# Two attentions of a four-stage transformer stack: the value products move from the end of a step to its middle and lag by two steps instead of one

## The chip, the cores and the metric

One core of one Trainium2 chip runs the whole program. The metric is the device time of one execution in microseconds; it is given as the median of several executions. The granted TensorE clock over the profiled execution is 0.971 of full speed, and 1.00 in both attention stages.

## What is computed

The reference is a stack of four residual layers, each `x = x + layernorm(f(layernorm(x)))`, over two sequences of 1024 tokens with 512 features:

```python
x = x + _layernorm(_L0_attn_ref(_layernorm(x), w_q, w_k, w_v, w_o))   # 32 heads of 16, full softmax
x = x + _layernorm(_L0_ffn_ref(_layernorm(x), ...))                   # gated MLP, 512 -> 1376 -> 512
x = x + _layernorm(_L1_attn_ref(_layernorm(x), Wqkv, Wo))             # 32 query heads, ONE key/value head, ALiBi, causal
x = x + _layernorm(_L1_ffn_ref(_layernorm(x), ...))                   # linear layer plus clamped low-rank adapter
# an attention, for each head: softmax(q k^T / 4 [+ alibi, causal]) v, then an output product
```

The change touches both attentions, and nothing of the rest.

## The kernel before

Each attention is one call of `attention`, with tag B (layer 0, full) or G (layer 1, `causal`). Its main loop runs over **steps**. Four heads form a group (`it`, 16 of them: 2 sequences x 8 groups). A group's queries come in two halves of 512; one group and half is a **turn** `t = 2*it + half` (32 turns). A turn is cut into key tiles `kt` of 128 keys. One step is one (`it`, `half`, `kt`). Layer 0 has 8 steps in each turn, 256 in all, all of full width. Layer 1 has 4 steps in an even turn and 8 in an odd one, 192 in all; tiles on the diagonal are narrower (512, 384, 256 or 128 queries), wide and narrow steps alternate, and each diagonal key product is followed by two small mask products (`mask_keys`, L1043).

The work of a step, by engine:

- **TensorE, key products** (`key_scores`, L1032), four a step, one for each head: scores with keys on partitions, into a ring of `n_st = 3` PSUM banks (`st_ps`). Key product n waits until ScalarE has used number n-3 (`st_used`). It is complete, and `st_made` counts it, only after its masks if it has any.
- **ScalarE, exponentials** (`exps`, L906), one for each key product, in the same order, into `probs`, a ring of three steps (`ring = 3`).
- **TensorE, row products** (`row_scores`, L1021): scores with queries on partitions, for the row maxima of a turn that comes later. A unit is one head and 128 queries; a wide one has two products (parts 0 and 1). Four PSUM banks (`s_ps`) hold two wide units. In layer 0 a step has two units.
- **VectorE, maxima** (`maximum`: L952 in layer 0, L949 in layer 1), one for each unit; it frees the unit's banks (`maxed`).
- **TensorE, value products** (`values`, L1065): for each of four heads `o_ps += v_ones x probs`, all into the one bank 7 that gathers a turn's output. Each is written to the trace as two instructions, so a step's group has 8.
- Once in a turn: `copy_o(t)` copies the finished bank 7 to SBUF (VectorE L958 in layer 0, ScalarE L913 in layer 1). The first value product of the next turn (`kt == 0`) waits for it (`o_out`). `invert` (L964) is a small reciprocal on VectorE, in the second step of a turn.
- Once in a turn: `turn_max(t)` (L1053) transposes the maxima through the same ring `st_ps`, ScalarE reads it twice (`take_max`, L895 and L896), and four small DMAs (L701, on SP's queue) write the maxima as rows of the query stack; the first key product of turn t waits for them (`m_rows`). In layer 0 `turn_max` stands at the end of the sixth step of the turn before, so the first key product that needs it is two whole steps later.

Key and row products contract over about 50 rows and sit in the upper or the lower half of the array; `step_order` interleaves the two halves so that one of each half can run at once. A step of layer 0 is, in order, K0, R(A,0), K1, R(A,1), R(B,0), K2, R(B,1), K3 with units A and B; the value products of the step before follow at the end. The order within each engine is this written order; semaphores alone tie the engines together. In the last 8 steps of an attention there are no row products, and pieces of the output product (`out.tile_piece`, L74 to L76) take their place.

In the main loop of TensorE before the change:

```python
for kind, *which in step_order(i):
    ...                       # key, row and mask products of step i
if i:
    values(i - 1)             # waits st_used for the exponentials of step i-1, o_out where kt == 0
...
for t in turn_after.get(i, ()):
    turn_max(t)
```

Of the kernel before, what the change touches and what calls it, by code (L numbers as in the profile page):

```python
# [47 lines left out]
SIDES = P // SIDE  # L48
GS = GH // SIDES
LEAD = 3400  # L50
TILES_AHEAD = 4
ROW_FIXED, STEP_FIXED = 140, 370
LOWEST = -3.0e38
# [440 lines left out]
def attention(nc, fixed_sb, step_sb, turn_sb, sems, tag, banks, causal, proj, qparts, kparts, vrows, out, nxt, turns,  # L494
# [23 lines left out]
    s_ps, st_ps, o_ps = banks[:, 0:4, :], banks[:, 4:4 + n_st, :], banks[:, 7, :]  # L518
# [61 lines left out]
    def step_order(i):  # L580

        _, _, _, first, diagonal = steps[i]
        keys = [[h for h in range(GH) if h // GS == u] for u in range(SIDES)]
        lists = [[], []]
        todo = units_at[i]

        def add_key(u):  # L590
            h = keys[u].pop(0)
            lists[u] += [("key", h)] + [("mask", h, a) for a in range(2) if diagonal]

        for j, n in enumerate(todo):
            u = units[n][2] // GS
            lists[u] += [("row", n, k) for k in range(len(row_parts(*units[n][:2])))]
            for _ in range(GH * (j + 1) // len(todo) - GH * j // len(todo)):
                add_key(1 - u if keys[1 - u] else u)
        while any(keys):
            add_key(0 if len(keys[0]) >= len(keys[1]) else 1)  # L600

        out, free = [], [0, 0]
        while any(lists):
            u = 0 if lists[0] and (free[0] <= free[1] or not lists[1]) else 1
            item = lists[u].pop(0)
            out.append(item)
            if item[0] == "row":
                x, y = row_parts(*units[item[1]][:2])[item[2]]
                free[u] += y - x
            else:  # L610
                free[u] += HALF - first if item[0] == "key" else SIDE * (item[2] + 1)
        return out
# [15 lines left out]
    tiles_ahead = TILES_AHEAD  # L628
# [47 lines left out]
    with nc.Block() as block:  # L676
# [210 lines left out]
        @block.scalar  # L887
        def _(act):
            def take_max(t):
                n = where["max", t, 0]  # L890
                act.wait_ge(st_made, n + 1)
                if t:
                    act.wait_ge(m_rows, n_rows * t)
                turned = st_ps[0:UNITS, n % n_st, 0:P]
                act.activation(mparts[:, 0, :], turned, ACT.Copy, scale=-1.0).then_inc(m_high, 1)  # L895
                act.activation(mrow[:, :], turned, ACT.Copy, scale=-1.0).then_inc(st_used, 1)  # L896

            def exps(i):
                first = steps[i][3]
                order = heads_of(i)  # L900
                for h in order:
                    n = where["exp", i, h]
                    act.wait_ge(st_made, n + 1)
                    if h == order[0] and i >= ring:
                        act.wait_ge(pv_done, i - ring + 1)
                    act.activation(probs[:, (i % ring) * GH + h, first:HALF], st_ps[:, n % n_st, first:HALF],  # L906
                                   ACT.Exp).then_inc(st_used, 1)

            def copy_o(t):
                act.wait_ge(pv_done, first_of[t + 1])  # L910
                if t >= 3:
                    act.wait_ge(o_stored, 16 * (t - 2))
                act.activation(ob[:, t % 3, :], o_ps[:, :], ACT.Copy).then_inc(o_out, 1)  # L913

            proj.scalar(act)
            for kind, n, *c in ahead:
                if kind == "out" and c[0] == DC - 1:
                    proj.copy(act, NB - 1, n)
                elif kind == "turn":
                    take_max(n)  # L920
            for i, (it, half, kt, *_) in enumerate(steps):
                exps(i)
                if causal and kt == 0 and i:
                    copy_o(2 * it + half - 1)
                for t in turn_after.get(i, ()):
                    take_max(t)
                if tile_at(i, -2) is not None:
                    out.tile_high(act, tile_at(i, -2), divided, TURNS // BATCH // 2)
            if causal:
                copy_o(TURNS - 1)  # L930
            for t in range(tiles_ahead + 2, NT):
                out.tile_high(act, t, divided, TURNS // BATCH // 2)
                nxt.scalar_tile(act, t)
            nxt.scalar(act, out)

        @block.vector
        def _(dve):
# [39 lines left out]
            for i, (it, half, kt, *_) in enumerate(steps):  # L977
                for n in units_at[i]:
                    maximum(n)
                if i - 1 == first_of[2 * it + half] and 2 * it + half >= 3:  # L980
                    invert(2 * it + half - 3)
                if not causal and kt == 0 and i:
                    copy_o(2 * it + half - 1)
                if i - first_of[last] in (3, 5):
                    invert(last - 2 + (i - first_of[last] - 3) // 2)
                if tile_at(i, -1) is not None:
                    out.tile_low(dve, tile_at(i, -1))
                if tile_at(i, 2) is not None:
                    out.tile_stats(dve, tile_at(i, 2), s_ps)
                if tile_at(i, 3) is not None:  # L990
                    out.tile_norm(dve, tile_at(i, 3), s_ps)
                if tile_at(i, 4) in range(TB - 1):
                    nxt.stats_tile(dve, tile_at(i, 4), out)
# [17 lines left out]
        def _(pe):  # L1011
# [75 lines left out]
            for i, (it, half, kt, *_) in enumerate(steps):  # L1087
                if kt == 0:
                    pe.wait_ge(m_rows, n_rows * (2 * it + half + 1))
                if i == tiles_at:  # L1090
                    pe.wait_ge(maxed, len(units))
                tile, odd = divmod(i - tiles_at, 2)
                keys, tile = 0, tile if 0 <= tile < tiles_ahead else None
                for kind, *which in step_order(i):
                    if kind == "row":
                        row_scores(*which)
                    elif kind == "key":
                        key_scores(i, *which)
                        keys += 1
                        if keys == 2 and tile is not None:  # L1100
                            out.tile_piece(pe, tile, 2 * odd, s_ps)
                    else:
                        mask_keys(i, *which)
                if i:
                    values(i - 1)
                if tile is not None:
                    out.tile_piece(pe, tile, 2 * odd + 1, s_ps)
                for t in turn_after.get(i, ()):
                    turn_max(t)
            values(len(steps) - 1)  # L1110
            for t in range(tiles_ahead, NT):
                for c in range(DC):
                    out.tile_piece(pe, t, c, s_ps)
# [798 lines left out]
```

## Time and profile before

| | us |
|---|---|
| median of 3 executions | 2115.2 (2108.39 to 2123.23) |
| the profiled execution | 2104.26 |
| its span, first to last instruction | 2102.4 |
| main loop of attention B (first to last value product) | 192.9 to 874 |
| main loop of attention G | 1431.5 to 1914 |

Times are microseconds, unless marked ns. Engines: PE = TensorE matmul, PEld = TensorE weight load, DVE = VectorE, ACT = ScalarE, POOL = GpSimd, SP = SyncE with a queue of DMA issues. L12 is line 12 of the kernel. Matmuls are pipelined and overlap in pairs, so the start times of successive matmuls tell more than their durations, and a PE that is shown as busy may be waiting inside the shadow of the matmul before. `x8` after a group is the number of instructions in it; in square brackets stands the idle time of the engine before it and what ended it.

### The profile page before, as it was taken

The numbers are of one execution on the slowest core, as the hardware profiler recorded it, in microseconds if no ns is written. First come the engines' busy times: TensorE is split into PE (matmuls) and PEld (weight loads), VectorE is DVE, ScalarE is ACT, GpSimd is POOL, SyncE is SP. The second block draws the span as 40 slices with busy tenths as digits, with TensorE's granted clock in tenths as the row PEclk, the third lists the DMA queues.
The fourth block names the chain that finished last, engine by engine and source line by source line (L and its number), as shares of the span: only waits on it lengthen the run. The fifth ranks groups of instructions, "written<-read, shape, count | busy, mean of one in ns | idle before, by whom it ended". The sixth has DMA issues, their size and how long they took to land. (4 is left out here: it accounts for less than half of the span.)

```text
span 2102.4 us, 31922 instructions
## 1 busy us (share of the span) xinstructions
PE 1911.8 (91%) x11664; PEld 1083.4 (52%) x11664; DVE 1424.3 (68%) x2446; ACT 1141.7 (54%) x2393; POOL 225.7 (11%) x275
## 2 busy tenths in 40 slices
PE   5999999999999999969999998599999999998665
PEld 4865333333333333548888886464444444445454
DVE  5346999998999898554423333567787778765457
ACT  3224888887887788514222221226777777764133
POOL 0000000110000000330001010000012000014213
PEclk9999999999999999989999999799999999999788
DMA  6582544354435530262011000563445434412411
GB/s 206 157 192 72 79 76 92 65 85 78 77 57 86 79 73 22 69 200 91 1 41 36 5 21 11 167 154 80 85 112 92 91 78 87 91 45 88 150 41 60
DMA packets 133820, 178.18 MB, mean 85 GB/s; under 512 B 50164, under 2 KB 61300, under 8 KB 133520
## 3 DMA queue, kind: packets, MB, share of 16 engines
q1 hardware_dynamic: 131360, 169.09, 35.3%
q0 software_dynamic: 2304, 7.06, 1.1%
q8 instruction: 92, 1.51, 0.3%
q14 instruction: 64, 0.52, 0.1%
HBM read 111.21 MB, written 64.36 MB: 84 GB/s over the span
## 5 line engine op out<-in xcount | busy, mean ns | idle before, releaser
L952 DVE TENSOR_REDUCE maxesB<-banksB 128x1 f32<-128x1024 f32 x512 | 602.0, 1216 | 86.2 <-PE banksB L1021 86.1
L906 ACT ACTIVATE probsB<-banksB 128x512 f32<-128x512 f32 x1024 | 529.6, 602 | 127.9 <-PE banksB L1032 127.8
L949 DVE CUSTOM_DVE_ANT_0 junkG<-banksG,rampG 128x896 bf16<-128x896 f32 (+7 forms) x512 | 367.9, 756 | 98.4 <-PE banksG L1021 92.9
L1032 PE MATMUL banksB<-q_stackB,k_stackB 50*128 50x512 f32 x1024 | 403.1, 470 | 4.8 <-ACT probsB L906 2.1
L906 ACT ACTIVATE probsG<-banksG 128x512 f32<-128x512 f32 (+3 forms) x768 | 326.1, 492 | 117.1 <-PE banksG L1043 66.1
L1021 PE MATMUL banksB<-k_stackB,q_stackB 48*128 48x512 f32 x1024 | 343.6, 441 | 3.8
L1032 PEld LDWEIGHTS banksB<-q_stackB,k_stackB 50*128 50x128 f32 x1024 | 166.5, 184 | 265.6 <-ACT probsB L906 231.3
L1032 PE MATMUL banksG<-q_stackG,k_stackG 54*128 54x512 f32 (+3 forms) x768 | 258.4, 412 | 22.4 <-ACT probsG L906 16.5
L1065 PE MATMUL banksB<-probsB,v_onesB 128*32 128x512 f32 x2048 | 273.6, 606 | 0.0
L1021 PE MATMUL banksG<-k_stackG,q_stackG 52*128 52x512 f32 (+3 forms) x768 | 247.0, 407 | 9.1 <-DVE maxesG L949 8.8
L1021 PEld LDWEIGHTS banksB<-k_stackB,q_stackB 48*128 48x128 f32 x1024 | 153.5, 185 | 85.5 <-DVE maxesB L952 74.7
L1032 PEld LDWEIGHTS banksG<-q_stackG,k_stackG 54*128 54x128 f32 x768 | 126.0, 185 | 104.7 <-ACT probsG L906 75.8
L1021 PEld LDWEIGHTS banksG<-k_stackG,q_stackG 52*128 52x128 f32 x768 | 125.3, 185 | 94.8 <-DVE maxesG L949 63.6
L1452 DVE SCALAR_TENSOR_TENSOR hD<-banksB,suD,siluD 128x512 f32<-128x512 f32 (+1 forms) x44 | 33.0, 750 | 207.7 <-PE banksB L76 190.9
L1065 PE MATMUL banksG<-probsG,v_onesG 128*32 128x512 f32 (+3 forms) x1536 | 164.5, 500 | 0.1
L1043 PE MATMUL banksG<-masks,halves 64*128 64x64 bf16 (+1 forms) x1024 | 119.0, 210 | 0.0
L1422 ACT ACTIVATE siluD<-banksB,sgD 128x512 f32<-128x512 f32 (+1 forms) x44 | 30.3, 688 | 131.4 <-PE banksB L76 131.3
L1431 ACT ACTIVATE hhD<-hD 128x512 fp32r<-128x512 f32 (+1 forms) x44 | 27.8, 632 | 114.4 <-DVE hD L1452 114.4
L76 PE MATMUL banksB<-xhTD,wgu2D 128*128 128x512 f32 x192 | 74.9, 390 | 0.0
L829 POOL TENSOR_TENSOR mpartsB<-mrowB,mpartsB 16x128 fp32r<-16x128 f32 x32 | 14.5, 453 | 562.4 <-ACT mrowB L896 562.4
L74 PE MATMUL banksB<-xhTD,wgu2D 128*128 128x512 f32 x192 | 74.8, 390 | 0.0
L75 PE MATMUL banksB<-xlTD,wgu2D 128*128 128x512 f32 x192 | 74.7, 389 | 0.0
(279 smaller groups left out, 2788.6 us busy)
## 6 DMA issues: line engine op xcount, KB each, us to landing
q_stackB<-q_parts SPq DMA_DIRECT2D x96, 128.0 KB, 7.1
k_stackB<-k_parts SPq DMA_DIRECT2D x96, 128.0 KB, 7.5
q_stackG<-q_parts SPq DMA_DIRECT2D x96, 128.0 KB
q_parts<-partsA SPq DMA_DIRECT2D x16, 512.0 KB, 4.1
k_parts<-partsA SPq DMA_DIRECT2D x16, 512.0 KB, 2.8
turns<-o_copyB SPq DMA_DIRECT2D x32, 256.0 KB, 2.2
q_parts<-partsF SPq DMA_DIRECT2D x16, 512.0 KB, 2.8
turns<-o_copyG SPq DMA_DIRECT2D x32, 256.0 KB
```

The source lines that it names most:

```text
L74: pe.matmul(out, left[0], right[0], start=start, stop=False)
L75: pe.matmul(out, left[0], right[1], start=False, stop=False)
L76: return pe.matmul(out, left[1], right[0], start=False, stop=stop)
L906: act.activation(probs[:, (i % ring) * GH + h, first:HALF], st_ps[:, n % n_st, first:HALF], ACT.Exp).then_inc(st_used, 1)
L949: dve.tensor_tensor_reduce(junk[:, n % JUNK, 0:width], scores, ramp[:, SEQ - width:SEQ], 1.0, LOWEST, ALU.add, ALU.max, out).then_inc(maxe ...
L952: dve.reduce_max(out, scores, AX.X).then_inc(maxed, 1)
L1021: ins = pe.matmul(s_ps[:, slot_of[n] + part, 0:b - a], qst[at, it % 3, half, h % GS, qt * P:(qt + 1) * P], kst[at, it % 3, h % kh, a:b], s ...
L1032: ins = pe.matmul(st_ps[:, n % n_st, first:HALF], kst[at, it % 3, h % kh, kt * P:(kt + 1) * P], qst[at, it % 3, half, h % GS, first:HALF], ...
L1043: ins = pe.matmul(st_ps[:, n % n_st, first:first + wide], halves[at, a, :], masks[at, a, 0:wide], start=False, stop=a == 1)
L1065: ins = pe.matmul(o_ps[32 * h:32 * h + 32, first:HALF], vone[:, it % 2, kt, h % vh, :], probs[:, (i % ring) * GH + h, first:HALF], start=k ...
L1422: act.activation(self.silu[0:k, :], self.g_ps[0:k, :], ACT.Silu, scale=self.sg[0:k, j:j + 1]).then_inc(self.silu_out, 1)
L1452: dve.scalar_tensor_tensor(out=self.h[0:k, :], in0=self.u_ps[0:k, :], scalar=self.su[0:k, j:j + 1], in1=self.silu[0:k, :], op0=ALU.mult, o ...
```

## The change

The value products leave the end of the step. They now stand in its middle, ahead of the third key product (or ahead of part 0 of a row unit where that stands directly before the third key product), and they are those of step i-2. After the loop the last two steps' value products follow. The first output piece of a step follows the value products. `copy_o(t)` moves from the first step of the next turn to its second, in ACT's and in DVE's order. The rings keep their sizes.

```diff
+VALUES_BEHIND = 2
...
-                if causal and kt == 0 and i:
+                if causal and i - first_of[2 * it + half] == 1 and 2 * it + half:
                     copy_o(2 * it + half - 1)
...
                 if i - 1 == first_of[2 * it + half] and 2 * it + half >= 3:
                     invert(2 * it + half - 3)
-                if not causal and kt == 0 and i:
+                if not causal and i - first_of[2 * it + half] == 1 and 2 * it + half:
                     copy_o(2 * it + half - 1)
...
-                keys, tile = 0, tile if 0 <= tile < tiles_ahead else None
-                for kind, *which in step_order(i):
+                tile = tile if 0 <= tile < tiles_ahead else None
+                order = step_order(i)
+                middle = next(n for n, item in enumerate(order) if item[0] == "key" and sum(
+                    o[0] == "key" for o in order[:n]) == 2)
+                if middle and order[middle - 1][0] == "row" and order[middle - 1][2] == 0:
+                    middle -= 1
+                for n, (kind, *which) in enumerate(order):
+                    if n == middle:
+                        if i >= VALUES_BEHIND:
+                            values(i - VALUES_BEHIND)
+                        if tile is not None:
+                            out.tile_piece(pe, tile, 2 * odd, s_ps)
                     if kind == "row":
                         row_scores(*which)
                     elif kind == "key":
                         key_scores(i, *which)
-                        keys += 1
-                        if keys == 2 and tile is not None:
-                            out.tile_piece(pe, tile, 2 * odd, s_ps)
                     else:
                         mask_keys(i, *which)
-                if i:
-                    values(i - 1)
                 if tile is not None:
                     out.tile_piece(pe, tile, 2 * odd + 1, s_ps)
                 for t in turn_after.get(i, ()):
                     turn_max(t)
-            values(len(steps) - 1)
+            for i in range(len(steps) - VALUES_BEHIND, len(steps)):
+                values(i)
```

## Rows read from the trace of the kernel before

**Rows 1.** Busy time of each engine in the two attention loops (columns are in the header).
```profile
core 0: us, PE busy (x) PEld busy (x) DVE busy (x) ACT busy (x) POOL busy (x), PEclk, DMA share, GB/s
192.90:854.90 662.00, 655.72 (x4048) 242.69 (x4047) 593.98 (x558) 529.27 (x1061) 54.46 (x80) 1.00 0.41 71
1431.40:1907.00 475.60, 446.41 (x4081) 221.74 (x4083) 360.69 (x998) 345.72 (x849) 54.18 (x86) 1.00 0.41 83
```

**Rows 2.** Timeline of PE over two steps of attention B: start, length, what.
```profile
571.76 0.50 PE L1032 MATMUL banksB<-q_stackB,k_stackB 50*128 50x512 f32 x1
...
572.70 0.39 PE L1021 MATMUL banksB<-k_stackB,q_stackB 48*128 48x512 f32 x1
572.95 0.50 PE L1032 MATMUL banksB<-q_stackB,k_stackB 50*128 50x512 f32 x1
573.38 1.07 PE L1065 MATMUL banksB<-probsB,v_onesB 128*32 128x512 f32 x8
574.38 0.50 PE L1032 MATMUL banksB<-q_stackB,k_stackB 50*128 50x512 f32 x1
...
575.56 0.39 PE L1021 MATMUL banksB<-k_stackB,q_stackB 48*128 48x512 f32 x1
575.57 0.49 PE L1032 MATMUL banksB<-q_stackB,k_stackB 50*128 50x512 f32 x1
575.98 1.06 PE L1065 MATMUL banksB<-probsB,v_onesB 128*32 128x512 f32 x8
```

**Rows 3.** Timeline of ACT over the same step.
```profile
572.30 2.06 ACT L906 ACTIVATE probsB<-banksB 128x512 f32<-128x512 f32 x4 [0.55 <-PE banksB L1032]
574.91 0.60 ACT L906 ACTIVATE probsB<-banksB 128x512 f32<-128x512 f32 x1 [0.55 <-PE banksB L1032]
```

**Rows 4.** Timeline of DVE: a plain step, then around a turn's copy and reciprocal.
```profile
506.86 2.36 DVE L952 TENSOR_REDUCE maxesB<-banksB 128x1 f32<-128x1024 f32 x2 [0.25 <-PE banksB L1021]
...
572.23 0.68 DVE L958 COPY o_copyB<-banksB 128x512 f32<-128x512 f32 x1
572.83 2.35 DVE L952 TENSOR_REDUCE maxesB<-banksB 128x1 f32<-128x1024 f32 x2
575.09 0.24 DVE L964 RECIPROCAL o_recipB<-o_sumsB 128x16 f32<-128x16 f32 x1
575.25 2.29 DVE L952 TENSOR_REDUCE maxesB<-banksB 128x1 f32<-128x1024 f32 x2
```

**Rows 5.** From the page's groups: all maxima of attention B, busy time, mean ns of one.
```profile
L952 DVE TENSOR_REDUCE maxesB<-banksB 128x1 f32<-128x1024 f32 x512 | 602.0, 1216 | 86.2 <-PE banksB L1021 86.1
```

**Rows 6.** Timeline of PE where a turn's maxima are turned (L1053).
```profile
562.76 1.06 PE L1065 MATMUL banksB<-probsB,v_onesB 128*32 128x512 f32 x8
563.64 0.38 PE L1053 MATMUL banksB<-ident,maxesB 128*16 128x128 f32 x2
563.95 0.49 PE L1032 MATMUL banksB<-q_stackB,k_stackB 50*128 50x512 f32 x1
...
565.55 1.06 PE L1065 MATMUL banksB<-probsB,v_onesB 128*32 128x512 f32 x8
```

**Rows 7.** Timeline: the maxima read by ACT, and the weight load of the turn's first key product.
```profile
500.96 0.27 ACT L895 ACTIVATE mpartsB<-banksB 16x128 fp32r<-16x128 f32 x1 [0.31 <-PE banksB L1053]
...
506.06 0.18 PEld L1032 LDWEIGHTS banksB<-q_stackB,k_stackB 50*128 50x128 f32 x1 [0.84 <-DMA q_stackB<-mpartsB]
```

**Rows 8.** Waits of PE from 192.9 to 1000: in total, times, longest (a single row).
```profile
PE banksB L1032 <- DMA q_stackB<-mpartsB: 1.8, 3, 1.0
```

**Rows 9.** Timeline of PE in attention G, steps 100 and, further down, 107.
```profile
1675.59 0.40 PE L1032 MATMUL banksG<-q_stackG,k_stackG 54*128 54x512 f32 x1
...
1676.57 0.49 PE L1021 MATMUL banksG<-k_stackG,q_stackG 52*128 52x512 f32 x1 [0.53 <-DVE maxesG L949]
1676.57 0.50 PE L1032 MATMUL banksG<-q_stackG,k_stackG 54*128 54x512 f32 x1
...
1692.46 0.55 PE L1032 MATMUL banksG<-q_stackG,k_stackG 54*128 54x512 f32 x2
1692.78 0.26 PE L1043 MATMUL banksG<-masks,halves 64*128 64x64 bf16 x2
```

## The prediction

> **What bounds the kernel now.** I read first the busy time in stretches of the two loops that the change touches [rows 1]. In attention B PE shows 655.7 of 662.0 us, DVE 594.0, ACT 529.3; in attention G 446.4 of 475.6, with DVE at 360.7 and ACT at 345.7. The granted clock is 1.00 in both. That looks like a loop bound by TensorE, but a busy PE can hide a wait in the shadow of the matmul before, so I went on to the timelines of PE, ACT and DVE over one step of B [rows 2 to 4].
>
> The first key product starts at 571.76, the fourth at 572.95, the value products at 573.38, the next step at 574.38: 1.19 + 0.43 + 1.00 = 2.62 (2.61 by the later rows). The 1.19 is no matmul work. The fourth key product follows 0.25 after the row product before it, alone, where the others run in pairs. It is gated by the ring of three banks: the exponentials of the step start at 572.30, 0.54 after the first key product, and the first one (0.60 long, row at 574.91) ends at 572.90. The fourth key product starts 0.05 later [rows 2, 3]. So the circle that sets attention B is **first key product, its exponential, fourth key product, value products, first key product again**: 0.54 + 0.60 + 0.05 + 0.43 + 1.00 = 2.62. DVE is close behind: its two maxima take 2.36 and it idles 0.25 in a step [rows 4].
>
> **The change in the steady state: no gain.** One has to count what stands between two groups of value products. Before: K0 K1 K2 K3 of one step. After: K2 K3 of step i, then K0 K1 of step i+1. It is four key products again, over the same three banks. The first of them (K2) must be exponentiated before the fourth (K1 of the next step) may start, and the value products stand behind the fourth as before. The circle is the same, turned by half a step: 1.19 + 0.43 + 1.00. The fourth is now followed by its row partner; after such a pair at 575.56/575.57 the value products start at 575.98, 0.42 later, as after a lone fourth product [rows 2]. The two-step lag ends no wait, for the value products at the end of a step did not wait either: the exponentials of step i-1 are done before the fourth key product of step i may start, since that one needs an exponential of step i. On DVE the two units follow each other as before: B then A', both with rows ready in time. I take 0 for the about 245 plain steps of B. Bounds: DVE's floor of 2.36 against 2.61 would give -0.25 a step; above, nothing in the rows makes it longer.
>
> **`turn_max`, 31 times in the steps of B.** It takes a place in the ring of three. Before, it stood right behind the value products, and its step took 565.55 - 562.76 = 2.79 against 2.61 [rows 6]. After, it stands behind K3 and between the value products, so five products share three banks: K2, K3, turn, K0', K1'. K0' waits for the exponential of K2 (1.19 after the value products), K1' for that of K3. Four exponentials take 2.06, of which the last is 0.60, so they follow each other by (2.06 - 0.60)/3 = 0.49 [rows 3]; K1' starts at 1.19 + 0.49 = 1.68, and the step takes 1.68 + 0.43 + 1.00 = 3.11. That is 0.32 more than 2.79: **31 x 0.32 = +9.9 us**. The two pairs before it and the turn itself lie under the wait.
>
> **`copy_o`, the part that costs.** Let zero be the end of the last value products of a turn, now in the middle of the next turn's second step. The bank must be copied before the next group, naturally at 1.19 + 0.43 = 1.62. DVE does the copy after both units of that second step, and the second unit's row products stand on PE behind those very value products. In a plain step the first products start at 506.06 and DVE starts on their unit at 506.86, so 0.80 after the pair [rows 4, 7]. One maximum takes 1.22, two of them 2.35, so the next instruction starts 2.35 - 1.22 = 1.13 after a maximum [rows 4, 5]; the reciprocal takes 575.25 - 575.09 = 0.16 until the next, the copy 0.68 [rows 4]: 0.80 + 1.13 + 0.16 + 0.68 = 2.77, and 0.05 until PE goes. The value products start at 2.82 instead of 1.62, so PE stands for **1.20**. Before, the copy stood behind units whose rows were ahead of the value products, and it started and ended under the next step's four key products: the steps around a copy take the same 2.61 [rows 2]. Queued behind the waiting value products are unit B's rows and K2, K3; for them wait DVE, which idles, and ACT, which has emptied its queue. Nothing pays the time back, since the circle above starts anew from the end of the value products. There are 31 copies inside the loop; the last of them falls among the steps with output pieces, which are long enough: **30 x 1.20 = +36 us**. Bounds: 0 if the copy were hidden; above, one more maximum ahead of the copy would make it 1.20 + 1.13 = 2.33, 70 us, but DVE's order has none there.
>
> What stands behind a waiting product waits too: at step 100 of G a row product waits 0.53 for DVE, and the key product behind it, which has another bank, starts with it at 1676.57, not earlier [rows 9]. The Trainium skill, TensorE: Matmul & The Clock Gate, section "Step-by-step: what each phase is for", states that on PE only weight loads are pulled ahead and matmuls keep program order. By that rule the trace agrees; if matmuls could pass, the 36 us would be 0.
>
> **Other queues.** The maxima's way to the key rows: ACT reads them at 500.96, the first key product that needs them starts at 506.06, and the DMA ended within the 0.84 before it [rows 7]; in 3 turns of 32 it was late, 1.8 us in all [rows 8]. After the change ACT has the exponentials of K2 and K3 still ahead of it when the turn comes (about 0.4 later, relative to the turn), while the key product comes 0.2 later; the margin shrinks by 0.2. I take 0, at most 31 x 0.2 = 6 us. SP's store of an output waits for copies two turns old; POOL's spread of v, and the split of maxima behind it, wait for value products half a step later, many steps ahead of their use: 0. At the end the same number of value products is left: 0 to 2 us.
>
> **Attention G** has the same ring, narrower steps and the copy on ACT. The copy follows four short exponentials of a 128-wide step there, so the value products wait 0.1 or nothing. Two things are new. In wide diagonal steps the middle falls between a key product and its masks, so its exponential starts only after the value products. In step 107 the masks come 0.32 after the key product and take 0.26 [rows 9]: the product is complete about 0.5 after the value products, two exponentials follow it (0.60 + 0.49) before the fourth key product may start, at 1.69 instead of 1.19, a loss of 0.5; I give the narrower step 105 half of it; the next step, with a turn behind it, loses about 0.3 by the rule of five in three banks. Against that, the wait for DVE in step 100, 1676.57 against about 1675.9 for a pair in its turn (0.3 after 1675.59), 0.7, now has value products in its place [rows 9], and alternating wide and narrow halves evens out 0.2. Sum 1.05 - 0.9 = +0.15 for each of 16 groups: **+2 us**; bounds: the losses alone +17, the gains alone -14.
>
> **Sum:** 9.9 + 36 + 2 = +48 us on the profiled 2104.3: 2152. The median of the runs is 2115.2, 10.9 above the profiled execution, so the forecast is **2163 us** (+2.3%).
>
> **Rivals.**
> 1. *The circle does get shorter* (not slower than now): if value products in the middle cover the exponentials of K0 and K1, a step falls to DVE's 2.36. For it: ACT idles 0.55 in a step and DVE 0.25 [rows 3, 4]. Against it: four keys on three banks as before. 245 x -0.25 = -61, +48: 2102. It decides from about 0.2 a step on (48/245).
> 2. *The copy stays hidden*: unit B's maximum comes early enough. 9.9 + 2: 2127. Against it: its rows are behind the value products.
> 3. *The maxima arrive late*: the copy's and turn's delays on ACT and SP make the first key product of each turn wait 0.2 to 0.5: 2163 + 6 to 15 = 2169 to 2178. For it: the 0.84 margin is an upper bound only [rows 7].
> 4. *Attention G loses the whole of its bound*: 2163 + 15 = 2178.
>
> **How the numbers follow.** Forecast 0.70, rival 1 0.07, rival 2 0.08, rival 3 0.08, rival 4 0.07. The median of the runs moves by some 8 us by itself. The range runs from 2136, which leaves out rivals 1 and 2, to 2186, which takes in 3 and 4 with that spread. A measurement of this kernel tells about 1%, 21 us, from no change. Slower by over 1% is above 2136: forecast, 3 and 4, 0.85. Within 1%: rival 2 and most of rival 1, 0.11. Faster 0.04.
>
> **What would show it.** In the changed trace: value groups in B 2.61 apart in plain steps, about 3.1 around L1053 and about 3.8 once a turn, with a wait of some 1.2 for DVE L958 before the first value product of a turn (30 times). DVE idle about 0.7 after it. In G 29.6 us a group, give or take 1. The prediction is wrong if plain steps of B are shorter than 2.55, or if no wait for L958 appears.

## The result, and the profile after

| | before | after |
|---|---|---|
| median (4 runs each) | 2112.58 us (2108.39 to 2123.23) | 2178.85 us (2172.84 to 2179.91) |
| the profiled execution | 2104.26 us | 2172.84 us |
| its span | 2102.4 us | 2171.0 us |

The ratio is 1.032, with a 95% interval of 1.028 to 1.036: the change makes the kernel 3.2% slower. The forecast was 2163, 2.3% slower, in a range from 2136 to 2186: the measured time lies within the range, 16 us above the forecast.

In the line numbers of the changed kernel everything behind the new constant is one higher: key products L1033, row products L1022, value products L1066, `turn_max` L1054, maxima L953, copies L959, reciprocals L965, exponentials L907.

First the page of the changed kernel: its first line, the busy time of the engines, and the granted clock in 40 slices of the span.

```profile
span 2171.0 us, 31922 instructions
...
PE 1939.0 (89%) x11664; PEld 1108.1 (51%) x11664; DVE 1432.1 (66%) x2446; ACT 1129.2 (52%) x2393; POOL 226.6 (10%) x275
...
PEclk9998999999899999998999999699999999999888
```

The number of instructions is the same, and the busy time of DVE and ACT is within 13 us of before (1424.3 and 1141.7). The span is 68.6 us longer. Where that is shows in the starts of the value groups. From the first key product to the end of the last value product attention B took 685.6 us before (188.5 to 874.1) and 751.1 after (189.0 to 940.1): **+65.5**. Attention G took 487.5 and 488.0: +0.5. The stages in front of, between and behind them make the other 2.6.

A turn of B in the changed kernel, on PE; the copy's wait, then plain steps (start, length, what, and in brackets what ended the idle time):

```profile
445.58 1.07 PE L1066 MATMUL banksB<-probsB,v_onesB 128*32 128x512 f32 x8
...
447.78 0.50 PE L1033 MATMUL banksB<-q_stackB,k_stackB 50*128 50x512 f32 x1
447.78 0.50 PE L1022 MATMUL banksB<-k_stackB,q_stackB 48*128 48x512 f32 x1
...
449.34 1.06 PE L1066 MATMUL banksB<-probsB,v_onesB 128*32 128x512 f32 x8 [1.06 <-DVE o_copyB L959]
...
451.96 1.06 PE L1066 MATMUL banksB<-probsB,v_onesB 128*32 128x512 f32 x8
```

and DVE over the same stretch:

```profile
447.36 1.22 DVE L953 TENSOR_REDUCE maxesB<-banksB 128x1 f32<-128x1024 f32 x1 [0.28 <-PE banksB L1022]
448.50 0.24 DVE L965 RECIPROCAL o_recipB<-o_sumsB 128x16 f32<-128x16 f32 x1
448.66 0.63 DVE L959 COPY o_copyB<-banksB 128x512 f32<-128x512 f32 x1
449.20 1.21 DVE L953 TENSOR_REDUCE maxesB<-banksB 128x1 f32<-128x1024 f32 x1
451.11 2.35 DVE L953 TENSOR_REDUCE maxesB<-banksB 128x1 f32<-128x1024 f32 x2 [0.69 <-PE banksB L1022]
```

The plain interval is 451.96 - 449.34 = 2.62, next to 2.60 to 2.61 before [rows 2]. The interval with the copy in it is 449.34 - 445.58 = 3.76. The last key product before the value products starts at 447.78, so they could have followed at 448.21; they start 1.13 later, 0.05 after the copy's end at 449.29. DVE came to the copy only after unit B's maximum (447.36) and the reciprocal. It then did one more maximum (449.20), whose rows stood ahead of the value products, and stood for 0.69, since the rows of the next unit stood behind them. In every second turn the value products start about 0.1 after the copy instead of 0.05, and there the profile names no engine as what ended the wait but "issue" (time in which it sees nothing waited for): about half of the 30 waits are named so.

The step with `turn_max` (L1054) in it:

```profile
457.20 1.07 PE L1066 MATMUL banksB<-probsB,v_onesB 128*32 128x512 f32 x8
...
458.86 0.39 PE L1054 MATMUL banksB<-ident,maxesB 128*16 128x128 f32 x2
459.38 0.50 PE L1033 MATMUL banksB<-q_stackB,k_stackB 50*128 50x512 f32 x1
...
459.87 0.49 PE L1033 MATMUL banksB<-q_stackB,k_stackB 50*128 50x512 f32 x1
...
460.30 1.07 PE L1066 MATMUL banksB<-probsB,v_onesB 128*32 128x512 f32 x8
```

460.30 - 457.20 = 3.10, against 2.79 before [rows 6]; K0' starts 1.19 after the value products' end and K1' 1.68 after it, as in the working.

What the working did not have is the clock. Busy time in two neighbouring turns of B (the third number from the right is the granted clock, PEclk):

```profile
core 0: us, PE busy (x) PEld busy (x) DVE busy (x) ACT busy (x) POOL busy (x), PEclk, DMA share, GB/s
424.40:449.30 24.90, 23.00 (x130) 8.50 (x130) 19.59 (x19) 16.80 (x34) 3.53 (x4) 0.86 0.26 55
449.30:471.90 22.60, 20.25 (x130) 7.72 (x130) 19.69 (x19) 16.79 (x34) 3.41 (x5) 1.00 0.48 84
```

Both turns hold the same work and one copy wait each. The first has a clock of 0.86: the granted clock went down from 2.4 to 1.2 GHz for a few microseconds right after the wait that ended at 424.44. The value products of that stretch:

```profile
424.44 1.53 PE L1066 MATMUL banksB<-probsB,v_onesB 128*32 128x512 f32 x8 [1.11 <-issue]
...
428.12 1.94 PE L1066 MATMUL banksB<-probsB,v_onesB 128*32 128x512 f32 x8
...
432.01 1.07 PE L1066 MATMUL banksB<-probsB,v_onesB 128*32 128x512 f32 x8
```

The first two intervals are 3.68 and 3.89 instead of 2.62. Eight of the 30 copy waits are followed by such a stretch.

The 65.5 us of B, from the intervals of the profiled execution:

| | us |
|---|---|
| 30 intervals with a copy, 3.64 to 3.80, mean 3.76, instead of 2.61 | +34.5 |
| 31 with `turn_max`, 3.10 instead of 2.80 | +9.5 |
| intervals lengthened by the low clock after eight copy waits | +17.6 |
| the first steps of B, at the low clock for longer than before | +3.1 |
| late maxima of the kernel before (three intervals, longer by 0.2 to 1.0 [rows 8]), absent here | -2.0 |
| plain steps (2.617 instead of 2.605, some 2 us) and both ends of the loop | +2.8 |

### The profile page after: what moved, and what is told of

It is laid out like the page before. It is cut to its first block and busy times, and to the rows that moved or that the text cites. A ratio compares the mean times of both kernels' runs of the same rounds, so it can differ in the third digit from the quotient of the medians.

```text
span 2171.0 us, 31922 instructions
## 1 busy us (share of the span) xinstructions
PE 1939.0 (89%) x11664; PEld 1108.1 (51%) x11664; DVE 1432.1 (66%) x2446; ACT 1129.2 (52%) x2393; POOL 226.6 (10%) x275
## 5 line engine op out<-in xcount | busy, mean ns | idle before, releaser
L953 DVE TENSOR_REDUCE maxesB<-banksB 128x1 f32<-128x1024 f32 x512 | 609.2, 1220 | 142.8 <-PE banksB L1022 128.2
L907 ACT ACTIVATE probsB<-banksB 128x512 f32<-128x512 f32 x1024 | 531.7, 600 | 208.6 <-PE banksB L1033 208.6
L1033 PE MATMUL banksB<-q_stackB,k_stackB 50*128 50x512 f32 x1024 | 390.2, 467 | 37.0 <-ACT probsB L907 13.4
L1022 PE MATMUL banksB<-k_stackB,q_stackB 48*128 48x512 f32 x1024 | 408.2, 477 | 0.0
L907 ACT ACTIVATE probsG<-banksG 128x512 f32<-128x512 f32 (+3 forms) x768 | 325.0, 491 | 138.4 <-PE banksG L1044 98.4
L1066 PE MATMUL banksB<-probsB,v_onesB 128*32 128x512 f32 x2048 | 286.0, 631 | 32.4 <-issue 16.5
L1022 PEld LDWEIGHTS banksB<-k_stackB,q_stackB 48*128 48x128 f32 x1024 | 175.9, 192 | 229.8 <-DVE maxesB L953 165.7
L1033 PE MATMUL banksG<-q_stackG,k_stackG 54*128 54x512 f32 (+3 forms) x768 | 262.7, 411 | 9.8 <-ACT probsG L907 8.1
L1033 PEld LDWEIGHTS banksB<-q_stackB,k_stackB 50*128 50x128 f32 x1024 | 174.4, 192 | 152.2 <-ACT probsB L907 135.1
L1022 PE MATMUL banksG<-k_stackG,q_stackG 52*128 52x512 f32 (+3 forms) x768 | 245.3, 399 | 1.1 <-DVE partsF L408 0.2
L1033 PEld LDWEIGHTS banksG<-q_stackG,k_stackG 54*128 54x128 f32 x768 | 129.2, 185 | 133.5 <-ACT probsG L907 121.2
L1066 PE MATMUL banksG<-probsG,v_onesG 128*32 128x512 f32 (+3 forms) x1536 | 164.5, 500 | 2.5 <-issue 2.3
L1022 PEld LDWEIGHTS banksG<-k_stackG,q_stackG 52*128 52x128 f32 x768 | 125.2, 186 | 61.1 <-DVE maxesG L950 42.6
L1044 PE MATMUL banksG<-masks,halves 64*128 64x128 bf16 (+1 forms) x1024 | 128.4, 210 | 0.0
L1066 PEld LDWEIGHTS banksB<-probsB,v_onesB 128*32 128x32 f32 x2048 | 41.2, 109 | 99.3 <-ACT probsB L907 42.2
```

The costliest lines, as they stand in the source:

```text
L953: dve.reduce_max(out, scores, AX.X).then_inc(maxed, 1)
L1022: ins = pe.matmul(s_ps[:, slot_of[n] + part, 0:b - a], qst[at, it % 3, half, h % GS, qt * P:(qt + 1) * P], kst[at, it % 3, h % kh, a:b], s ...
L1033: ins = pe.matmul(st_ps[:, n % n_st, first:HALF], kst[at, it % 3, h % kh, kt * P:(kt + 1) * P], qst[at, it % 3, half, h % GS, first:HALF], ...
L1044: ins = pe.matmul(st_ps[:, n % n_st, first:first + wide], halves[at, a, :], masks[at, a, 0:wide], start=False, stop=a == 1)
L1066: ins = pe.matmul(o_ps[32 * h:32 * h + 32, first:HALF], vone[:, it % 2, kt, h % vh, :], probs[:, (i % ring) * GH + h, first:HALF], start=k ...
```

## Experiments

Where an experiment has a single execution its time is given beside the 2173 to 2180 of the changed kernel, and the reading goes by the intervals of its trace. Those of plain steps and of steps with a turn repeat within 0.02 from turn to turn; those at a copy alternate between two values 0.05 apart.

### The copy's place in DVE's order

```diff
 # the changed kernel, attention B, DVE, second step of a turn
-maximum(A); maximum(B); invert; copy_o(t)
+maximum(A); copy_o(t); maximum(B); invert
```

> The changed kernel with one thing moved: in attention B VectorE copies the finished turn between the two maxima of the step (after the unit whose rows stand ahead of the value products), not after both. My theory, the copy waits for unit B's maximum: the interval between value groups at a turn falls from about 3.77 to 2.6-2.8, no wait for L959-like copies is left, and about 30 x 1.15 = 35 us go. On the clock: if the falls to half clock in attention B (8 stretches, about 20 us) come from the waits for the copy, they go too and the time is about 2122; if they come from elsewhere, they stay and the time is about 2143. Rival, the wait is for the value products or the bank itself: the interval stays at 3.7 and the time at 2179.

Measured: 2121.74. All intervals with a copy are 2.61 to 2.63. DVE, then PE, in the same place of a turn:

```profile
497.62 0.68 DVE L959 COPY o_copyB<-banksB 128x512 f32<-128x512 f32 x1
498.22 1.21 DVE L953 TENSOR_REDUCE maxesB<-banksB 128x1 f32<-128x1024 f32 x1
```

```profile
496.20 1.07 PE L1070 MATMUL banksB<-probsB,v_onesB 128*32 128x512 f32 x8
...
498.83 1.07 PE L1070 MATMUL banksB<-probsB,v_onesB 128*32 128x512 f32 x8
```

The copy now ends at 498.30, 0.5 before the value products are due, and unit B's maximum is 0.25 later without harm. The rival falls: neither the bank nor the value products themselves made the wait. And the low stretches are gone with it, as the first of the two cases for the clock had it: after its first steps attention B is at a clock of 1.00 (below). From its first key product to its last value product B takes 700.7 instead of 751.1, so the wait and the clock together are 50 us of the 65.5.

### `turn_max` right behind the value products

```diff
 # the changed kernel, attention B: ring order and ACT's order moved along
-K0 R K1 R | values | R K2 R K3 | turn_max
+K0 R K1 R | values | turn_max | R K2 R K3
```

> The changed kernel with one thing moved: in attention B turn_max stands right behind the value products in the middle of the step, ahead of K2, and takes its place in the ring of three accordingly. My theory, five products on three banks with the turn third of them: the step with a turn falls from 3.11 to about 2.80 (as in the kernel before), 31 x 0.31 = 9.6 us less, 2169 if the clock falls alike. Rival, the 0.3 comes from the turn itself on TensorE: it stays at 3.1 and the time at 2179.

Measured: 2164.20, and the step with a turn takes 2.81 in every turn instead of 3.10. The rival falls; five products in three banks with the turn as the third of them is what cost 0.3. In this execution, too, eight low stretches follow copy waits.

### The lag alone

```diff
 # the kernel before, both attentions; copies in the second step of a turn
-if i: values(i - 1)          # end of step i
+if i >= 2: values(i - 2)     # end of step i
```

> The kernel before with the lag of two steps alone: value products still at the end of a step, those of step i-2, with the copies in the second step of a turn. My theory, the lag neither helps nor harms: 2.61 for plain steps, 2.80 with a turn, 2.61 at a copy, clock as in the kernel before, 2112 +- 6. Rival, the lag of two costs (the ring of three steps of probs holds ScalarE back, or the copy comes late): more than 2125, with plain steps longer than 2.62. Other rival, the lag frees something: below 2100.

Measured: 2128.63. In B the forecast holds: plain 2.60 to 2.61, with a turn 2.81, at a copy 2.61, and B as a whole 687.3 against 685.6. The lag neither gives nor takes there. The sum misses, and not because of B: attention G took 507.0 instead of 487.5. In its undisturbed groups G was even faster (29.35 instead of 29.57 a group), but G began with the granted clock at 1.2 GHz for 31 us (7 before), and its first group took 37.2 instead of 30.8. Among the first five groups DVE then waited four times, 9.9 us in all, for DMAs of the sums (once, 1.9, before), and the clock fell twice more; it fell a last time in the steps with output pieces. The longest of these waits, on DVE:

```profile
1580.41 0.25 DVE L964 RECIPROCAL o_recipG<-o_sumsG 128x16 f32<-128x16 f32 x1 [3.48 <-DMA o_sumsG<-turns]
```

The long low start is not the lag's: late_copy and later_copy (below), whose G is that of the kernel before, begin it with 24 us at 1.2 GHz. The late DMAs stay open: every other trace here has at most 1.9 us of that wait in G, those with a lag of two in G too, but this is the only execution with that lag and the value products at the end of a step.

### The place alone

```diff
 # the changed kernel; copies in the first step of a turn
-VALUES_BEHIND = 2
+VALUES_BEHIND = 1
```

> The changed kernel with a lag of one step: value products in the middle of step i are those of step i-1, copies in the first step of a turn. My theory, the place costs and the lag hardly matters: plain steps 2.61 to 2.68 (the exponential of K3 of the step before ends about when the value products are due), 3.1 with a turn, 3.7 to 3.8 at a copy, in all 2170 to 2200. Rival, the lag of two is what makes the middle bearable: plain steps at 3 or more, 2280 or more.

Measured: 2178.78, as slow as the change. Plain steps of B 2.67, with a turn 3.10, at a copy 3.63 to 3.69. So in B the middle place carries the losses whatever the lag, and the lag of two buys back 0.06 in a plain step; about 185 steps are plain, so some 11 us. B as a whole is 11.4 shorter than in the change all the same (739.7 against 751.1): in this run the clock fell at none of the copies. Attention G makes up for it. A group of G takes 30.8 instead of 29.90, and G as a whole 503.7 instead of 488.0, so there the lag of two is worth 15.7 us. Once in a group the profile of place_alone names a wait of 0.55 of the value products for ScalarE's copy (7.2 us in 13 waits from 1520 to 1900), which the change has not; the rest of the 0.9 a group was not traced. That the two times agree is chance.

Its trace also shows how a wait for several semaphores can be put down to the wrong one. First DVE, then PE:

```profile
216.10 0.68 DVE L959 COPY o_copyB<-banksB 128x512 f32<-128x512 f32 x1
```

```profile
216.83 1.07 PE L1066 MATMUL banksB<-probsB,v_onesB 128*32 128x512 f32 x8 [0.95 <-ACT probsB L907]
```

The row names ACT, but the value products start 0.05 after the copy's end, and only at copies; the exponentials they need belong to the step before.

### The same wait in the old place

```diff
 # the kernel before, attention B, DVE
-first step of a turn:  maximum(A); maximum(B); copy_o(t)
+second step of a turn: maximum(A); copy_o(t); maximum(B)      # late_copy
+second step of a turn: maximum(A); maximum(B); copy_o(t)      # later_copy
```

> The kernel before with one thing moved: in attention B the copy of a finished turn stands between the two maxima of the turn's second step (before: behind both maxima of the first). The value products stay where they were. The first value group of a turn then waits until about 0.80 + 1.13 + 0.68 + 0.05 = 2.66 instead of 1.61. My theory: one interval in eight grows from 2.61 to about 3.6, 30 x 1.0 = 30 us more, whatever the place of the value products. On the clock: place_alone waits about 1.0 at a copy and shows no low stretch there, the changed kernel waits about 1.15 and shows eight; if the length of the wait decides, this one has none and lands at 2145. If the clock falls with any wait of a turn, 2160 or more.

> The same as late_copy with the copy behind both maxima of the turn's second step: the wait is about 0.80 + 1.13 + 1.13 + 0.16 + 0.68 + 0.05 = 3.95 instead of 1.61, so about 2.3 each turn, 70 us more. My theory on the clock, longer waits let it fall: low stretches in attention B in most turns, and a time over 2115 + 70 + 20 = 2205. Rival, the falls in the changed kernel came from the middle place of the value products and not from the wait: none here, and 2185.

Measured: late_copy 2158.92, later_copy 2249.78. The intervals at a copy are 3.67 to 3.72 and 4.81 to 4.96, so waits of 1.07 to 1.11 and 2.2 to 2.35 against 1.0 and 2.3 worked out, with value products at the end of the step. Busy time over attention B, with the clock as the third number from the right; late_copy:

```profile
205.00:921.00 716.00, 683.54 (x4087) 255.99 (x4085) 600.62 (x566) 535.92 (x1073) 61.26 (x88) 0.97 0.38 67
```

the same row of later_copy:

```profile
205.00:1010.00 805.00, 735.61 (x4070) 278.74 (x4066) 596.86 (x564) 534.18 (x1069) 60.86 (x87) 0.88 0.34 60
```

of the changed kernel:

```profile
210.00:940.00 730.00, 662.07 (x4075) 250.08 (x4067) 599.39 (x564) 527.81 (x1067) 60.88 (x88) 0.96 0.37 66
```

of copy_between:

```profile
210.00:889.00 679.00, 644.77 (x4074) 248.94 (x4066) 594.15 (x564) 527.74 (x1066) 60.21 (x87) 1.00 0.41 71
```

and of place_alone:

```profile
205.00:925.00 720.00, 646.37 (x4076) 242.29 (x4068) 601.23 (x567) 528.63 (x1070) 59.54 (x86) 1.00 0.38 67
```

Both kernels have value products in the old place and the clock falls in both, and with the middle place and no wait (copy_between) it does not: the middle place is not its cause, the wait is. later_copy's theory of the clock held. What I expected of the clock in late_copy was wrong: I had set 1.0 as harmless and it fell after some waits of 1.1. In order of the wait: none (copy_between) and 1.0 (place_alone) 1.00, 1.1 (late_copy) 0.97 with 6 low stretches, 1.15 (the change) 0.96 with 8, 2.3 (later_copy) 0.88 with 26. These are single executions, and 1.0 and 1.1 lie close together. Why one wait of 1.1 is followed by the low clock and the next one is not, these runs do not tell.

### The masks behind the value products, in attention G

```diff
 # the changed kernel, diagonal steps of G, e.g. step 107
-R K2 R M2 M2 K3 | values | K0 M3 M3 R M0 M0 K1 ...
+R K2 R M2 M2 K3 K0 M3 M3 R M0 M0 | values | K1 ...             # whole_masks
+R K2 R M2 M2 K3 M3 M3 | values | K0 R M0 M0 K1 ...             # masks_ahead
```

> The changed kernel with one thing moved: in diagonal steps of attention G the value products stand behind the masks of every key product that is ahead of them, so that no score waits behind them for its masks. My theory: the two intervals of 3.25 and 2.40 (steps 107 and 105) fall by 0.5 and 0.2, a group of G from 29.90 to about 29.2, 16 x 0.7 = 11 us less. Rival, the ring of three sets these intervals anyway, since three key products instead of two now stand ahead: a group stays within 0.2 of 29.90.

> The changed kernel with one thing moved: in diagonal steps of attention G the masks of the two key products ahead of the value products are issued ahead of the value products too; the same two key products stand ahead as in the change. My theory (a score that waits behind the value products for its masks costs the ring its head start): the intervals of 3.25 (step 107) and 2.40 (105) fall by about 0.5 and 0.2, a group of G from 29.90 to about 29.2, 11 us less in G. whole_masks, which kept masks together by putting three or four key products ahead, made a group 30.40; so a rival is that the masks are not the matter and only the count of key products ahead is: the group stays at 29.90. Attention B is as in the change (low stretches of the clock included).

Measured: whole_masks 2183.22 with 30.40 a group, masks_ahead 2169.78 with 29.68 a group, against 29.90 for the change. Both expectations miss in size. With three key products ahead of the value products a group is half a microsecond longer (intervals of 3.38 and 3.51 come in place of 2.55 and 2.62), so the place behind three key products has a loss of its own, larger than either the theory or its rival (within 0.2 of 29.90) allowed. With the masks alone ahead, the intervals of steps 105 and 103 fall from 2.40 to 2.11 and from 1.92 to 1.77, three others grow by 0.05 to 0.1, and the long one, 3.25, to which I had given 0.5 for its masks, does not move at all. Its trace says why. Around that interval in the changed kernel, on DVE and then on PE:

```profile
1761.02 1.23 DVE L950 CUSTOM_DVE_ANT_0 junkG<-banksG,rampG 128x1024 bf16<-128x1024 f32 x1
1762.16 0.08 DVE L950 DVE_READ_ACCUMULATOR2_ANT maxesG<- 128x1 f32 x1
```

```profile
1759.31 0.85 PE L1066 MATMUL banksG<-probsG,v_onesG 128*32 128x384 f32 x8
...
1761.29 0.98 PE L1033 MATMUL banksG<-q_stackG,k_stackG 54*128 54x512 f32 x2
1761.78 0.59 PE L1044 MATMUL banksG<-masks,halves 64*128 64x64 bf16 x4
1762.30 0.33 PE L1022 MATMUL banksG<-k_stackG,q_stackG 52*128 52x128 f32 x2
1762.56 1.06 PE L1066 MATMUL banksG<-probsG,v_onesG 128*32 128x512 f32 x8
```

Two narrow row products (1762.30) stand directly ahead of the value products and need a bank that the maximum of the last wide unit (1761.02 to 1762.25) frees. That unit's rows stand behind the value products before. In the trace of masks_ahead the same wait is named by the profile, DVE and then PE:

```profile
1760.09 1.23 DVE L950 CUSTOM_DVE_ANT_0 junkG<-banksG,rampG 128x1024 bf16<-128x1024 f32 x1 [0.26 <-PE banksG L1022]
```

```profile
1761.37 0.33 PE L1022 MATMUL banksG<-k_stackG,q_stackG 52*128 52x128 f32 x2 [0.33 <-DVE maxesG L950]
```

It is the copy's pattern once more.

### Both attentions mended, and G alone

```diff
 # mended: the changed kernel with copy_between, turn_behind_values and masks_ahead
 # only_g_mended: attention B as before; attention G as changed, with masks_ahead
```

> The changed kernel with all three things mended: the copy between the two maxima, turn_max right behind the value products, the masks ahead of them. Middle place and lag of two stay. My theory, place and lag neither give nor take: B as in the kernel before (2.61, 2.80 with a turn, 2.61 at a copy, no low stretches), G at 29.2 a group instead of 29.57: ratio to the kernel before 0.995 to 1.003. Rival, the middle place has a cost of its own that the three do not cover: 1.01 or more.

> Attention B as in the kernel before; attention G with value products in the middle, two steps behind, with the masks ahead of them. A try at beating both kernels. My theory: B unchanged, G 29.2 a group instead of 29.57, so some 6 us less, ratio 0.995 to 0.999. Rival, what G gains in its groups it loses at its ends: 1.000 or more.

Measured: mended 2108.36 (10 runs) against 2115.36, ratio 0.9981 (0.9964 to 0.9997); only_g_mended 2102.47 (6 runs), ratio 0.9946 (0.9922 to 0.9970). With the three mended, the losses of the change are gone: B's intervals are 2.62, 2.81 and 2.61. The middle place is not quite free in B all the same. mended lies 5.9 us above only_g_mended, whose B is that of before, and in their traces B takes 690.7 against 684.2: plain steps of 2.617 instead of 2.604, some 3 us, and first steps that are about 5 us longer, at 1.2 GHz until 206 instead of 194. Of the six traces with the middle place and the lag of two in B, five have the low clock until 206 to 210; in all others here it ends by 199. Why is open.

G's groups are 29.68, not the 29.2 expected, which is no gain over the 29.57 of before; in only_g_mended G gains at its ends (485.4 from its first key product to its last value product, against 487.5). That is 2 us, and the medians differ by 13. The traces cannot show the rest: the profiled execution of the kernel before (2104.26) is the fastest of all its executions on record, and the other executions of it, from 2106 to 2125, have granted clocks of 0.960 to 0.970, those of only_g_mended 0.969 to 0.970. What lowers the clock in the slower executions of before was not traced.

### Value products ahead of the narrow rows, in attention G

```diff
 # only_g_mended, plus
-if middle and order[middle - 1][0] == "row" and order[middle - 1][2] == 0:
+while middle and order[middle - 1][0] == "row" and order[middle - 1][2] == 0:
     middle -= 1
```

> only_g_mended with one word changed: the middle steps back over every first-part row product that stands directly ahead of it, not over one at most. Of attention G's steps that concerns the first of a group: its value products stand ahead of two 128-wide row products instead of behind them. Their banks are freed by the maximum of the last unit of the step before, whose rows stand behind the last value products. My theory: the interval of 3.26 there (unmoved by the masks) is that wait, in the way of the copy in B; it falls to about 2.9 and a group of G from 29.67 to about 29.3: ratio to the kernel before 0.991 to 0.995 against 0.9946 of only_g_mended. Rival, the interval is set by the ring of three and the exponentials: it stays above 3.15, and the ratio at 0.995.

Measured: 2099.03 (6 runs) against 2113.78, ratio 0.9934 (0.9916 to 0.9952). The interval of 3.26 is 2.60, the next one grows from 3.16 to 3.27, and a group of G takes 29.16, 0.41 less than before; G as a whole takes 477.3 against 487.5. The wait for the last wide unit's maximum was it; the ring's rival falls. The kernel is 0.5 to 0.8% faster than the one before; of the 15 us between the medians the traces show 5, since the profiled execution of before is its fastest. A direct ratio to only_g_mended was not measured, and the two intervals overlap; between their traces G is 8.0 us shorter.

### Splitting the value products

```diff
 # the kernel before, both attentions
-K0 R K1 R R K2 R K3 | values(i-1), four heads
+K0 R K1 R | values(i-1), two heads | R K2 R K3 | values(i-1), two heads
```

> A try at breaking the circle, from the kernel before: the value products of step i-1 are split, two heads in the middle of step i and two at its end (all four at the end where they begin a turn); masks stay with their key products; copies as before. My theory: the fourth key product then follows the first by 0.34 + 0.42 + 0.5 + 0.34 = 1.6 by its own place, later than the 1.19 of the ring, so a step is 0.34 + 0.42 + 0.50 twice = 2.52 instead of 2.61, in 7 of 8 steps: 215 x 0.09 = 19 us less in B, 2096 in all, plus or minus 10 from G. Rival, the circle is not what sets the step (TensorE's own pace is 2.6): a step with one more change between key and value products is 2.7, and the time 2135.

Measured: 2326.52, 10% slower, and both theories miss. PE:

```profile
503.06 1.05 PE L1067 MATMUL banksB<-probsB,v_onesB 128*32 128x512 f32 x4
504.04 0.49 PE L1021 MATMUL banksB<-k_stackB,q_stackB 48*128 48x512 f32 x1
...
504.38 0.39 PE L1021 MATMUL banksB<-k_stackB,q_stackB 48*128 48x512 f32 x1
...
504.71 1.05 PE L1067 MATMUL banksB<-probsB,v_onesB 128*32 128x512 f32 x4
```

The circle did open: between two groups the key and row products now take 504.71 - 504.04 = 0.67, no wait among them. But half a group (x4) takes 0.98, as long as a whole one (x8, 1.00 [rows 2]). My working had halved it. The four heads' value products write four different quarters of the partitions, and by these times they run side by side: two of them cost what four cost. A step is 2 x (0.67 + 0.98) = 3.30.

## Why the prediction was right or wrong

- **Steady state, no gain: right.** 2.62 after, 2.61 before. lag_alone and place_alone show the two halves of it: the lag alone changes nothing in B, the place alone costs 0.06 a step for lack of lag. Rival 1 (a shorter circle) is out: it asked for less than 2.55. Plain steps are 0.01 longer, some 2 us. The working counted about 245 plain steps; without the 31 with a turn and the 30 with a copy they are about 185, so rival 1's -61 was too large. The forecast did not rest on it.
- **`turn_max`: right in place and size.** 3.10 against a worked 3.11, +9.5 against +9.9 us; turn_behind_values takes it away.
- **`copy_o`: right in place, 4% too large in size.** In 28 of the 30 turns the wait is 1.12 to 1.18 against a worked 1.20 (the copy after a reciprocal is 0.63 long, not 0.68), in all +34.5 against +36 us. DVE's idle time, one maximum later, was 0.69, as forecast. Rival 2 (a hidden copy) did not come, though copy_between shows that it was one line away.
- **The step that failed is the clock**, which the sum left out: the term was missing. From the clock of 1.00 in both loops before [rows 1] I took, without saying so, a clock of 1.00 after, though I was adding thirty waits of PE of a length that the loop before had only once (the longest of three, 1.0 [rows 8]). It measured 17.6 us after the copies, with 3 more in the first steps, and it is the whole distance between the forecast's +48 and the measured +66 to +69. The 17.6 follow the waits and not the place of the value products: copy_between is without them, late_copy and later_copy have such stretches. The 3 do not follow the waits: copy_between and mended have them too.
- **That 2179 lies in the range is partly luck.** The room above the forecast was made for rivals 3 and 4 and for the spread of the runs; neither rival came, and a term that nobody had named filled it.
- **Attention G: the sum was near by luck, its parts partly wrong.** +0.5 us in all against +2. The groups are 29.90, +0.33 each, where +0.15 was worked out, and the ends of the loop, where the working had expected 0 to 2 us more, gave it back. Of the parts, the gain at step 100 came in kind but smaller (the interval there fell from 2.87 to 2.33, 0.54 instead of 0.7, with a loss of 0.2 in the next). The loss at step 105 came as worked out: 2.16 to 2.40, and masks_ahead takes it away. The interval at step 107 grew by 0.48, next to the 0.5 worked out, but not by its masks: masks_ahead leaves it at 3.26, and rows_behind takes 0.66 off it. The size was right by chance; the wait was for a bank behind DVE, which I had not looked for there.
- **The other queues: right.** The maxima's rows were never late in B after the change (three times before), SP and POOL cost nothing. Rivals 3 and 4 did not come.

## What to carry to other kernels

In a loop that is closed over several engines, count what stands between two occurrences of the blocking group: moving the group within the loop turns the circle and does not shorten it. What a move does change is which work stands ahead of each once-in-a-while item (the copy, the turn, a narrow unit) on the engine that serves it. Look for an item whose own queue holds, ahead of it, work that waits for something behind the moved group; each time, that costs what this work runs past the moment at which the group is due (the copy here ended 2.71 after the last value products, and the next were due at 1.63), and moving the item one place takes a few lines. A short wait that comes back every turn can cost more than its own length: price the clock too, here half of the waits again.

## What the runs showed of the hardware

- A wait of TensorE of about 1.1 us, once in 22 us, was followed by some microseconds at 1.2 GHz in 6 to 9 of 30 cases (late_copy 6, the change and turn_behind_values 8, whole_masks and masks_ahead 9), and waits of 2.3 us in 26: granted clock over the loop 0.97 and 0.96, and 0.88. With 30 waits of 1.0 (place_alone) or none (copy_between) it was 1.00. Nor did it fall after a single interval in B that a late DMA made 1.0 longer in the kernel before, or 1.2 longer in copy_between. In the changed kernel the low stretches added half as much again to what the waits themselves cost (17.6 to 34.5 us). The Trainium skill, TensorE: Matmul & The Clock Gate, section "HAM oscillation — how this bites in real kernels", describes idle gaps of TensorE, waits for DMAs of about 3 to 5 us, that throttle it again and again; the rows here agree in kind, with waits of a third of that and only after some of them.
- Value products of four heads, each 32 columns wide on its own quarter of the partitions, take 1.00 us together, and those of two heads 0.98.
